# Attention output: denominators as eight extra rows, placed by DMA and divided in place, instead of a turned output

## The reference, cut to what matters

```
scores = q @ k.T / sqrt(8)            # 1024 x 1024 (layer 1: keys after the query are masked)
attn   = softmax(scores, axis=-1) @ v # 1024 x 8
```

## Time and profile before

| | us |
|---|---|
| median of 3 runs | 2042.52 (2030.39 to 2044.81) |
| profiled execution, time | 2038.6 |
| profiled execution, span from first to last instruction | 2036.8 |
| attn0, units | about 141 to 538 |
| attn1, units | about 1355 to 1673 |
| PE busy | 1760.2 (86%) |
| DVE busy | 1468.9 (72%) |
| ACT busy | 1323.0 (65%) |
| POOL busy | 886.3 (44%) |

### The profile page before, as it was taken

How to read it: one execution, slowest core, us unless ns; L and a number is a source line. 1 busy time by engine, 2 the same in 40 slices (tenths; PEclk the granted TensorE clock), 3 DMA queues, 4 the chain that set the end, 5 groups by cost and what they waited for, 6 DMA issues and landing times. The chain is left out here.

```text
span 2036.8 us, 32306 instructions
## 1 busy us (share of the span) xinstructions
PE 1760.2 (86%) x10685; PEld 757.0 (37%) x10685; DVE 1468.9 (72%) x1473; ACT 1323.0 (65%) x2673; POOL 886.3 (44%) x567
## 2 busy tenths in 40 slices
PE   7779999999786777776776699899999999999996
PEld 2313333333344444444443333334444444233332
DVE  3678888887399999999999754556666624465456
ACT  4427777777799999989999534335555553543432
POOL 1076556664299999999999710000000001000000
PEclk8759999999998888888889899879999988999997
DMA  2354444442698888888888411322223000000000
GB/s 108 133 176 162 156 157 151 152 161 110 209 321 315 304 297 312 309 281 314 301 306 300 158 53 48 62 56 56 40 47 58 18 18 0 0 0 0 0 6 16
DMA packets 86546, 288.88 MB, mean 142 GB/s; under 512 B 11671, under 2 KB 15026, under 8 KB 84383
## 3 DMA queue, kind: packets, MB, share of 16 engines
q1 hardware_dynamic: 72319, 236.57, 36.3%
q0 software_dynamic: 13824, 50.34, 6.4%
q10 hardware_dynamic: 288, 0.45, 0.1%
HBM read 214.60 MB, written 61.21 MB: 135 GB/s over the span
## 5 line engine op out<-in xcount | busy, mean ns | idle before, releaser
L565 DVE TENSOR_REDUCE attn_mx<-banks 128x1 f32<-128x1024 f32 (+7 forms) x512 | 501.7, 990 | 148.0 <-PE banks L363 98.4
L1648 POOL TENSOR_TENSOR hc<-st,ct 128x1024 f32<-128x1024 f32 x256 | 597.7, 2368 | 6.4 <-DVE st L1607 6.0
L1607 DVE TENSOR_TENSOR_SCAN st<-da,banks 128x1024 f32<-128x1024 f32 x256 | 562.5, 2266 | 15.6 <-ACT da L1564 6.0
L517 ACT ACTIVATE attn_probs<-banks 128x512 f32<-128x512 f32 (+3 forms) x640 | 307.2, 533 | 193.8 <-PE banks L397 100.2
L1572 ACT ACTIVATE ut<-b_turned,mats 128x128 f32<-128x128 f32 x1024 | 311.6, 387 | 1.7
L1564 ACT ACTIVATE da<-dt,mats 128x1024 f32<-128x1024 f32 x256 | 282.6, 1138 | 25.3 <-DVE st L1607 18.6
L393 PE MATMUL banks<-attn_qa,attn_ka 75*128 75x512 bf16 (+3 forms) x896 | 268.9, 369 | 4.5 <-DMA attn_qa<-attn_mrow 2.5
L1489 PE MATMUL banks<-hc,onecol 128*32 128x512 f32 x1024 | 158.9, 696 | 102.1 <-POOL onecol L1646 79.6
L743 POOL TENSOR_TENSOR made_ahead<-b_turned,x_turned 128x1024 f32<-128x1024 f32 x96 | 183.8, 1914 | 110.9 <-DVE attn_mparts L580 59.1
L361 PE MATMUL banks<-attn_ka,attn_qa 64*128 64x512 bf16 (+3 forms) x512 | 197.1, 385 | 25.1 <-DVE attn_mx L565 21.0
L1465 PE MATMUL banks<-mats,ut 128*128 128x128 f32 x1024 | 162.5, 300 | 45.2 <-DVE st L1607 34.2
(11 more groups left out here) (442 smaller groups left out, 1977.9 us busy)
## 6 DMA issues: line engine op xcount, KB each, us to landing
dt<-dt_rows SPq DMA_DIRECT2D x256, 512.0 KB, 5.5
ahead<-made_ahead POOLq DMA_DIRECT2D x96, 512.0 KB, 3.4
ua<-ahead SPq DMA_DIRECT2D x96, 512.0 KB, 5.9
attn_qa<-q_lin SPq DMA_DIRECT2D x144, 64.0 KB
attn_qu<-attn_qa SPq DMA_DIRECT2D x16, 512.0 KB, 4.3
attn_ka<-k_lin SPq DMA_DIRECT2D x72, 64.0 KB
moe_w<-in_moe_w SPq DMA_DIRECT2D x2, 2048.0 KB, 11.5
mats<-in_mats SPq DMA_DIRECT2D x1, 2876.5 KB, 13.0
```

What stands on the lines that cost most here:

```text
L517: nc.scalar.activation(probs[s % 4][:, jj, c0:BLK], scores_exp[jj][:, c0:BLK], ACT.Exp, scale=scale).then_inc(probs_ready, 1)
L565: nc.vector.reduce_max(mx[:, qt, j:j + 1], scores_max[n % 2][:, 0:w], AX.X)\
L1607: nc.vector.tensor_tensor_scan(st[n % 4][:, :], da[n % 4][:, :], pair[:, :, :].rearrange("p h t -> p (h t)"), 0.0, ALU.mult, ALU.add).then ...
L1648: nc.gpsimd.tensor_tensor(hc[n % 8][:, :], st[n % 4][:, :], ct[:, b * SEQ:(b + 1) * SEQ], ALU.mult)\
```

## The change

Columns 8 to 15 of each head's `vst` are ones, not only column 8. `out_acc` thus has, for each head, 8 rows of output and 8 equal rows with the denominator. There are two banks of it, one for each half `qb` (banks 6 and 7), and `turn_max` borrows the one that is free (`turn_bank`). `turn_out`, the turning back after the last unit and its copies or adds are gone. After each `out_copy` SP sends 8 DMAs (`send_out`): for each head 8 rows of output to their place in `attn_t` and 8 rows of denominators to the same place in `dens` (this is `ssm_in`, which served as `attn_tok`). When all four groups of a sequence's half are in, DVE divides in place on 128 x 512: one reciprocal, one multiplication, in attn1 one addition to `x`. That is done four times per attention, all in the last unit or after it.

```diff
-                    nc.gpsimd.memset(vst[i][:, :, :, HD:HD + 1], 1.0).then_inc(vst_cleared, 1)
+                    nc.gpsimd.memset(vst[i][:, :, :, HD:2 * HD], 1.0).then_inc(vst_cleared, 1)
...
-        out_acc = k.bank[6]
-        turned = k.bank[7]
+        out_acc = [k.bank[6], k.bank[7]]
...
+        def turn_bank(i, half):
+            return out_acc[1 if i == 0 else half]
...
+                def send_out(i, qb):
+                    g, b = units[i]
+                    sp.wait_ge(osb_ready, 2 * i + qb + 1)
+                    t0 = b * SEQ + qb * BLK
+                    for j in range(4):
+                        rows = slice(32 * g + HD * j, 32 * g + HD * j + HD)
+                        for dst, o in ((attn_t, 32 * j), (dens, 32 * j + HD)):
+                            sp.dma_start(dst[rows, t0:t0 + BLK], osb[o:o + HD, :]).then_inc(osb_sent, 16)
...
                 for i in range(UNITS):
                     if 0 < i < UNITS - 1:
                         mirror(i + 1)
+                    if i > 0:
+                        send_out(i - 1, 1)
                     rows(i, 1)
                     if i + 2 < UNITS:
                         load(i + 2)
+                    send_out(i, 0)
                     if i + 1 < UNITS:
                         rows(i + 1, 0)
+                send_out(UNITS - 1, 1)
                 front.sync_third(sp)
...
                         if kt_slot == 0 or kt_slot == MID:
-                            pe.wait_ge(osb_ready, 2 * i + qb)
+                            if i > 0:
+                                pe.wait_ge(osb_ready, 2 * i - 1 + qb)
+                            pe.wait_ge(mrow_ready[qb], i + 1)
...
-                        if s == 3 and i > 0:
-                            turn_out(i - 1, 1)
-                        if s == MID + 3:
-                            turn_out(i, 0)
...
-                turn_out(UNITS - 1, 1)
-
-                pe.wait_ge(normed, 16)
-                for n in range(NBLK):
...
-                    for t in range(4):
-                        last = nc.tensor.matmul(k.bank[n % 2][:, sl(t, TILE)], attn_tok[:, 4 * n + t, :],
-                                                k.m("ident"), start=True, stop=True)
...
                 def out_copy(i, qb):
                     act.wait_ge(pv_done, NE * i + half_end[qb] + 1)
-                    act.wait_ge(oturned, 2 * i + qb)
-                    nc.scalar.copy(osb[:, :], out_acc[:, :]).then_inc(osb_ready, 1)
+                    if i > 0 or qb > 0:
+                        act.wait_ge(osb_sent, 128 * (2 * i + qb))
+                    nc.scalar.copy(osb[:, :], out_acc[qb][:, :]).then_inc(osb_ready, 1)
...
+                def out_norm(i, qb, n):
+                    dve.wait_ge(osb_sent, 128 * (2 * i + qb + 1))
+                    t0 = units[i][1] * SEQ + qb * BLK
+                    out, den = attn_t[:, t0:t0 + BLK], dens[:, t0:t0 + BLK]
+                    steps = 3 if residual else 2
+                    link(nc.vector.reciprocal(den, den), steps * n + 1, own_norm)
+                    link(nc.vector.tensor_tensor(out, out, den, ALU.mult), steps * n + 2, own_norm)
+                    if residual:
+                        x = k.x[:, t0:t0 + BLK]
+                        link(nc.vector.tensor_tensor(x, x, out, ALU.add), steps * n + 3, own_norm)
...
+                        if i == UNITS - 1 and s == MID - 3:
+                            for qb in range(2):
+                                out_norm(first_done, qb, qb)
+                        if i == UNITS - 1 and s == MID + 3:
+                            out_norm(i, 0, 2)
...
-                out_norm(UNITS - 1, 1)
-                for n in range(NBLK if residual else 0):
-                    dve.wait_ge(final_turned, n + 1)
-                    nc.vector.tensor_tensor(k.x[:, sl(n)], k.x[:, sl(n)], k.bank[n % 2][:, :], ALU.add)\
-                        .then_inc(final_copied, 1)
+                out_norm(UNITS - 1, 1, 3)
```

More of the change, by code:

```diff
@@ L138, with attention @@
 K_ORDER = [0, 1, 2] * 3
-def attention(k, tag, q_lin, k_lin, k_heads, v, causal, attn_t, front, units, tok=None, residual=False,
+def attention(k, tag, q_lin, k_lin, k_heads, v, causal, attn_t, front, units, dens, residual=False,
               probs=()):
@@ L249, in attention @@
         vstaged = k.sem(f"{tag}_vstaged")
+        first_done = max(i for i, u in enumerate(units) if u[1] != units[UNITS - 1][1])
         first_of = [min(i for i, u in enumerate(units) if u[1] == b) for b in range(2)]
@@ L369, in turn_max @@
                     pe.wait_ge(mparts_ready[half], i + 1)
+                    if half == 1:
+                        pe.wait_ge(mrow_ready[0], i + 1)
+                    elif i > 0:
+                        pe.wait_ge(mrow_ready[1], i)
+                    bank = turn_bank(i, half)
                     if i > 0:
-                        pe.wait_ge(normed, 2 * i - 1 + half)
+                        pe.wait_ge(osb_ready, 2 * i - 1 + half)
                     for t in range(4):
-                        last = nc.tensor.matmul(turned[0:12, sl(t, TILE)],
+                        last = nc.tensor.matmul(bank[0:12, sl(t, TILE)],
                                                 mparts[:, 4 * half + t, :, :].rearrange("p a j -> p (a j)"),
@@ L419, in pv_quad @@
                         last.then_inc(pv_done, 2)
[L421 to L426, removed]
-                        pe.wait_ge(mrow_ready[1], i + 1)
-                    elif i + 1 < UNITS:
-                        pe.wait_ge(mrow_ready[0], i + 2)
-                    for t in range(4):
-                        last = nc.tensor.matmul(turned[:, sl(t, TILE)], osb[:, sl(t, TILE)], k.m("ident"),
-                                                start=True, stop=True)
-                    last.then_inc(oturned, 1)
                 def first_pass(i, place):
@@ L448, in body @@
                             pe.wait_ge(mrow_ready[0 if s < 7 else 1], 1)
-                            filler(turned[:, :])
+                            filler(out_acc[1][:, :])
                         if odd and s > 1:
@@ L484, in _ @@
                     pv_quad(UNITS - 1, NE - 2, vst[1], part)
-                turn_out(UNITS - 1, 1)
-                pe.wait_ge(normed, 16)
-                for n in range(NBLK):
-                    if n >= 2:
-                        pe.wait_ge(final_copied, n - 1)
-                    for t in range(4):
-                        last = nc.tensor.matmul(k.bank[n % 2][:, sl(t, TILE)], attn_tok[:, 4 * n + t, :],
-                                                k.m("ident"), start=True, stop=True)
-                    last.then_inc(final_turned, 1)
             @block.scalar
@@ L549, in _ @@
                 out_copy(UNITS - 1, 1)
-                for n in range(NBLK if not residual else 0):
-                    act.wait_ge(final_turned, n + 1)
-                    nc.scalar.copy(attn_t[:, sl(n)], k.bank[n % 2][:, :]).then_inc(final_copied, 1)
             @block.vector
```

28 lines of the change are left out of this document (3 added, 25 removed).

## The result

The changed kernel takes 2093.98 us (median of 4 runs, 2061.1 to 2105.4), the one before 2037.93 in the same session (4 runs, 2030.39 to 2044.81). The ratio is 1.0164, interval 1.0103 to 1.0225: slower by 1.6%, where 0.8% faster was forecast, and far above the range of 2011 to 2040. The mean granted clock of TensorE goes with the time in all four: 0.897, 0.883, 0.871 and 0.871 of full speed from the shortest to the longest, against 0.923 in the profiled run before.

The account below looks back on a forecast made before the run. PE was taken to bound both attentions, at full clock. Gains of 37.1 us (33.5 + 3.6) less losses of 22.0 (0.4 + 13.8 + 4.3 + 3.5) gave net 15.1, forecast 2026 us, 8-in-10 range 2011 to 2040.

Parts of the forecast that it names:

- The step that failed: Inside both attentions: PE, busy nearly all the time, saves the removed turn_out in full, 1.09 us a place, 33.5 us gained.
- PE inside attn0: In attn0's units: without turn_out PE saves 1.09 us at each place; first to last copy about 18 us shorter.
- the two banks: In both attentions: PE no longer waits for ACT to empty the only output bank, 3.6 us gained.
- PE inside attn1: In attn1's units: without turn_out PE saves 1.09 us a place, 1.87 in the last unit; stretch about 18.6 us shorter.
- SP's queue inside the units: Sends of 5 us stand ahead of row DMAs in SP's queue; only attn1's last unit is late, 0.4 us lost.
- Rival (c): Inside attn1's units: sends hold up the row DMAs PE waits for, making the kernel slower, 2080 us; chance 0.10.
- The end of attn0: After attn0's last copy: SP's reload starts only behind the last send, 20.5 us to the next stage, 13.8 us lost.
- The end of attn1: After attn1's last copy: send issues, landing, reciprocal, multiplication and addition take 11.2 us, 4.3 us lost (1 to 9).
- The clock at refine's start: At refine's start: PE stands still about 12 us before it, so the clock falls to half, 3.5 us lost (0 to 6).
- The rivals: Whole kernel: shorter ends, about 2014 us, 0.28; saved time becoming waits, 2042, 0.12; sends delaying rows, 2080, 0.10; no gain, excluded.
- the forecast's 0.50: Whole kernel: chance 0.50 given to the forecast itself, a net gain of 8 to 20 us.

## Why the prediction was wrong

**The step that failed** is "So inside both attentions what PE no longer does is saved in full, until ACT or DVE has more work per slot than PE". It held in attn0 and failed in attn1. It priced `turn_out` by its time, at a clock that I took as given (1.00 in the earlier trace rows), and the clock term was set only where PE stops, at refine's start. But the clock was no constant of attn1: it depended on the work that was taken out. The experiments show it from both sides. Less turning in the kernel before brings the low clock (1.0279); four products, or 18 narrow ones of all rows, put in the old place take it away (1.0015, 0.9996); the same 18 with 16 rows don't (1.0693).

**What could have been seen.** The kernel before had some 24 us at 0.50 at the start of attn1, with PE busy in 22.00 of the 22 us shown above, that is, a low clock without any pause. Its code gave a sign too. Both kernels hold a `filler`, a product of 128 x 128 by 512 columns whose result nobody reads, ahead of and inside attn1's first unit; the last four, in the low stretch, begin at 1352.5 to 1361.6 us before the change and at 1355.2 to 1364.3 after it, take 0.6 us each instead of 0.38, and don't raise the clock by themselves. I had read only the stretch at 1643, which follows a pause of 1.8 us, and had made "PE stands still" the reason for a low clock. The Trainium skill, TensorE: Matmul & The Clock Gate, section "What's actually happening", says that the gate follows how busy PE has been. By that sentence a PE that is busy all the time should have the full clock in attn1. If busy means what the profile counts as busy, these traces disagree: 133.89 of 135 us at 0.50.

**Point by point.**
- PE inside attn0, and the two banks: right, -18.1 us (15 of the 30 turned outputs at 1.09, and half of 3.6). It is no luck: the stretch is 362.3 us in all three profiled kernels with the turned output and 344.1 or 344.2 in all that have the change and attn0's own score matmuls.
- PE inside attn1: as the change stands 54.4 us more, against 18.6 less forecast. Where the clock is mostly held there is a gain, but the traces don't give its full size. From the scan's last group to the last copy the kernels with zero rows need 506.5 us, 500.1 (with the split send) and 509.5 (zero rows on POOL's queue), where the kernel before with zero rows needs 517.3: 7.8 to 17.3 us less, and their clocks and waits are not quite alike.
- SP's queue inside the units: right in kind, 1.0 us of waiting more in the last unit where 0.4 was forecast. Rival (c) was on the right side for the wrong reason.
- The end of attn0: right, 21.0 against 20.5 us, and moving the reload gives back 10.9.
- The end of attn1: 12.4 against 11.2 us. The reciprocal, worked out of a 16-element one, was right at 3.35. The estimate from the Trainium skill, VectorE: DVE Perf Modes, section "First, the fixed hardware budget", with its repeat count of 8, was 4.5; the trace doesn't bear that out, and the measurement decides. The issues are 0.67 apart and not 0.6, and the landing is 2.05 and not 1.8.
- The clock at refine's start: right in kind, 2.5 us in the first eight matmuls; 3.5 forecast, since their 3.67 us were taken to double, and they took 6.15. In the whole stretch from refine to the end it can't be seen: 359.6 to 366.5 us in the kernels with the change, 361.1 to 363.6 in the three without.
- The rivals had no case for the clock inside an attention, so the chance of 0.10 for slower was too small. (A slip beside it: a quarter of the forecast's 0.50 is 0.125, and 0.10 was put into the sum for faster.)

**What stays open.** The 7.3 us before attn0's first copy: it begins at 168.5, 170.7 and 174.6 us in the three kernels with the turned output, and at 169.4 to 175.8 in those that have the change and the same front, so most of it is scatter between runs. Why the rows matter isn't shown, nor what makes the clock rise and fall at the very places where it does. Whether it is the rows as such or the share of the array that is fed was tried only with few weight columns (12 of 128, with all rows, did as well). Why attn0 holds its clock with the same 75-row matmuls wasn't tried; its units differ in having neither the mask products nor the narrow pieces of a causal mask, and they have 32 slots and not 24. Nor was it tried whether filling the max pass's 64-row matmuls would hold the clock as well.

## What to carry to other kernels

Before taking work from a bound PE, read the granted clock of each stage, and what PE did where it rises; a product of all 128 rows may be what holds it, and its time is then the price of the clock. If the clock falls after such a cut, try more rows in the matmuls that are already there, with zeros: here that cost PE almost nothing and turned 1.6% slower into 1.2% faster, together with the early reload and with the DMAs that write the zeros in a queue that nobody waits for. When a send to another stage is added at a block's end, put the independent reload ahead of it in the queue's order.

## What the runs showed of the hardware

- With PE busy by the profile for 133.89 of 135 us, the granted clock stayed at 0.50 (1.2 GHz). It isn't idleness alone that lowers it.
- Two kernels that differ only in the rows of 18 short matmuls per place (128 or 16) take 2040.5 and 2180.4 us; their clocks in 1400 to 1500 are 1.00 and 0.57. Zeros in the added rows of the score matmuls do it too (1.00 in the same stretch, without any extra matmul), though not everywhere: one of the kernels with 128 rows still has 18 us at 0.50.
- 24 products of float32 ahead of a pause, which leave PE still for 6.4 us, didn't keep the clock in the one run that had them: the eight matmuls after it take 6.24 us, and 6.15 after 13.1 us of stillness.
- A DMA of 16 KB within SBUF, from 8 partitions to 8, takes 0.62 us to issue; of eight in a row, the last has landed 2.05 us after its issue begins. A reciprocal of 128 x 512 float32 on DVE takes 3.35 us, five times a multiplication of that size (0.69).
